# Attention in a two-layer kernel: transpositions by halves of 64 rows, scores three units ahead, maxima ahead of copies

## What is computed

```python
def _L0_attn_ref(x, ln_g, ln_b, w_qkv, w_out):
    h, dh, ws = (8, 64, 128)          # heads, head size, window; n = 256 tokens
    xn = layernorm(x) * ln_g + ln_b
    qk, v = jnp.split(xn @ w_qkv.T, 2, axis=-1)
    bq = rope(to_buckets(qk) * dh ** (-0.5))
    bk = rope(_look_around(to_buckets(qk), -1.0))
    bv = _look_around(to_buckets(v), -1.0)
    sim = jnp.einsum('bwie,bwje->bwij', bq, bk)
    sim = jnp.where(mask[None], NEG, sim)     # pads and |i - j| > 128 are masked
    attn = jax.nn.softmax(sim, axis=-1)
    out = jnp.einsum('bwij,bwje->bwie', attn, bv)
    return out @ w_out.T
```

## Time and profile before

| | |
|---|---|
| median of 3 runs | 978.69 us (976.3 to 979.37) |
| the profiled execution, its own time | 976.32 us |
| its span, first to last instruction | 975.0 us |
| PE busy | 952.0 us, 98% |
| DVE, ACT, POOL busy | 666.1, 505.4, 434.6 us |
| weight loads busy | 633.6 us |
| granted TensorE clock | 0.999 of full speed |

### The profile page before, as it was taken

The page is one execution under the profiler, slowest core; times in us unless marked ns, Lnnn a source line. Parts: engine busy times, 40 slices in busy tenths (PEclk is TensorE's granted clock), DMA queues, the critical chain, the costliest instruction groups (busy, mean ns, idle before and its releaser), DMA issues.

```text
span 975.0 us, 13550 instructions
## 1 busy us (share of the span) xinstructions
PE 952.0 (98%) x4508; PEld 633.6 (65%) x4508; DVE 666.1 (68%) x1578; ACT 505.4 (52%) x1165; POOL 434.6 (45%) x343
## 2 busy tenths in 40 slices
PE   5899999999999999999999999999999999999998
PEld 3565566676666766677666766667666676656765
DVE  6957769687665876767866677757777477724943
ACT  3574783536746266462764537545465454745222
POOL 5858247551094401863036620566206651054443
PEclk9999999999999999999999999999999999999999
DMA  7050240613423034230442306332053220543061
GB/s 284 12 174 1 35 130 0 144 44 10 133 68 98 22 13 133 72 93 21 38 129 76 88 1 91 76 95 68 1 99 90 65 66 2 107 102 87 23 164 33
DMA packets 63381, 72.80 MB, mean 75 GB/s; under 512 B 33288, under 2 KB 34312, under 8 KB 62928
## 3 DMA queue, kind: packets, MB, share of 16 engines
q1 hardware_dynamic: 61744, 69.81, 31.0%
q10 hardware_dynamic: 1568, 2.13, 0.6%
HBM read 69.04 MB, written 2.88 MB: 74 GB/s over the span
## 4 chain that ended last, share of the span: by engine, by line
PE 88%; DVE 7%; ACT 2%; issue 2%; DMA 0%; POOL 0%; DVEq 0%; ACTq 0%
PE ps L648 12%; PE ps L765 12%; PE ps L503 10%; PE ps L505 9%; PE ps L504 9%; PE ps L557 6%; PE ps L570 6%; PE ps L584 5%; PE ps L656 3%; PE ps L740 2%; PE ps L773 1%; PE ps L498 1%; PE ps L538 1%; PE ps L729 1%; PE ps L528 1%
## 5 line engine op out<-in xcount | busy, mean ns | idle before, releaser
L1167 ACT ACTIVATE wide<-ps 128x512 f32<-128x512 f32 x136 | 80.9, 595 | 208.8 <-PE ps L505 208.2
L1093 ACT ACTIVATE pw<-ps,w_cols 128x512 f32<-128x512 f32 x144 | 98.5, 687 | 98.6 <-PE ps L505 97.2
L1054 ACT ACTIVATE pw<-ps,nmax 128x256 f32<-128x256 f32 x256 | 117.5, 473 | 51.1 <-DVE nmax L1420 46.6
L648 PE MATMUL ps<-pw,w_w 128*128 128x512 f32 x288 | 135.4, 592 | 0.0
L1907 POOL TENSOR_TENSOR atc<-atc,wide 128x512 f32<-128x512 f32 x64 | 82.0, 1282 | 119.8 <-DVE atc L1634 119.8
L1887 POOL TENSOR_TENSOR kr<-qks,w_rope 128x512 f32<-128x512 f32 x32 | 43.8, 1367 | 158.3 <-DVE qks L1398 158.2
L1436 DVE COPY pt<-ps 128x512 f32<-128x512 f32 x126 | 81.7, 679 | 26.5 <-PE ps L570 26.3
L503 PE MATMUL ps<-yc,eg 128*128 128x512 f32 x128 | 94.4, 738 | 0.0
L1907 POOL TENSOR_TENSOR pt<-pt,wide 128x512 f32<-128x512 f32 x48 | 61.7, 1284 | 66.4 <-DVE pt L1634 65.3
L1420 DVE TENSOR_REDUCE nmax<-ps 128x4 f32<-128x1024 f32 (+1 forms) x80 | 79.1, 1006 | 13.8 <-PE ps L557 13.7
L648 PEld LDWEIGHTS ps<-pw,w_w 128*128 128x128 f32 x288 | 53.5, 189 | 42.6 <-issue 37.7
(11 more groups left out here) (229 smaller groups left out, 2131.0 us busy)
## 6 DMA issues: line engine op xcount, KB each, us to landing
wb<-scratch SPq DMA_DIRECT2D x128, 256.0 KB, 4.0
wb<-scratch SPq DMA_DIRECT2D x32, 512.0 KB, 5.9
wide<-scratch SPq DMA_DIRECT2D x16, 512.0 KB, 5.7
xin<-in_x SPq DMA_DIRECT2D x8, 256.0 KB, 2.7
out<-wide SPq DMA_DIRECT2D x7, 256.0 KB, 10.3
wb<-in_w SPq DMA_DIRECT2D x1, 1152.0 KB, 8.5
w_w<-in_w SPq DMA_DIRECT2D x1, 1152.0 KB, 12.4
w_ed<-in_ed SPq DMA_DIRECT2D x1, 1024.0 KB, 15.7
```

Source lines behind the costliest of these rows:

```text
L648: pe.matmul(bank(k), w2[:, e, c, :], hid[:, n % 4, :], start=c == 0, stop=c == 1 and e < E0).then_inc(*DOWN0.one)
L1054: m = act.activation(pw[:, u % 2, j, :], ps[:, score_bank(u, par), qt * SEQ:(qt + 1) * SEQ], ACT.Exp, bias=nmax[:, u % 3, j:j + 1], scale= ...
L1093: act.activation(hid[:, n % 4, :], bank(UPS0[n % 2]), ACT.Gelu, bias=cols[:, C_B1 + 2 * e + c:C_B1 + 2 * e + c + 1], scale=1.0).then_inc(* ...
```

## The change

In steps 2 to 7 (`s > 1`):

- **PE** turns units 0 to 6 by `turn_by_halves`: rows 0 to 63 of all eight 128 by 128 blocks of a unit go to bank 0 and rows 64 to 127 to bank 7, each a product with 64 rows and 64 moving columns, the two halves alternating. One event of two counts ends a unit. Unit 7 keeps `turn`.
- **PE's order**: `scores(2)` comes first, then for each unit its turn and `scores(u + 3)`; `weigh_pair` 0 and 1 stay ahead of turns 3 and 5; `weigh_pair` 2 comes behind the first `up0_half`, ahead of turn 7.
- **Masks**, in all steps: written by products of 64 rows, in the same halves of the array as the scores that follow. Each head's bank takes two such products, so `short_ident` and `mask` get a second copy, shifted by 64 columns, made at the start (`masks_further_on` on POOL, two more copies on ACT). `scores` now waits for both banks ahead of the first mask.
- **DVE**: `maxima(u + 2)` ahead of the copies of unit u. `pt_copy_half` copies a bank of one half into 64-wide pieces of `pt_of(u)`.
- **ACT**: `out_cols` of pairs 0 and 1 one unit later, behind units 4 and 6.

```diff
-        short_ident = sb("short_ident", [P, P], BF16)
-        mask = sb("mask", [P, 2, P], BF16)
+        short_ident = sb("short_ident", [P, 2, P], BF16)
+        mask = sb("mask", [P, 2, 2, P], BF16)
...
             def scores(s, u):
                 p, g = u // G, u % G
                 banks = [score_bank(u, par) for par in range(2)]
                 for b in banks:
                     take(b)
-                    pe.matmul(ps[:, b, P:3 * P], short_ident[:, :],
-                              mask[:, :, :].rearrange("p q k -> p (q k)"), start=True, stop=False,
-                              skip_group_check=True)
+                w.wait_ge(*MASKS.at(0))
+
+                for h in range(2):
+                    for par, b in enumerate(banks):
+                        rows = half_rows(par)
+                        pe.matmul(ps[:, b, P:3 * P], short_ident[rows, h, :],
+                                  mask[rows, h, :, :].rearrange("p q k -> p (q k)"), start=h == 0, stop=False,
+                                  skip_group_check=True)
...
+            def turn_by_halves(s, u):
+
+                for par, k in enumerate(TURN_BANKS):
+                    w.wait_ge(*EXPS.at(s, 2 * u + par))
+                    take(k)
+                for j in range(8):
+                    par, kt, qt = j // 4, j // 2 % 2, j % 2
+                    for h, k in enumerate(TURN_BANKS):
+                        m = pe.transpose(bank(k)[:, j * 64:j * 64 + 64],
+                                         pw[half_rows(h), u % 2, 2 * par + qt, kt * P:(kt + 1) * P],
+                                         ident[half_rows(h), half_rows(h)])
+                m.then_inc(TRANSPOSED.sem, 2)
+                for h, k in enumerate(TURN_BANKS):
+                    freed[k] = PT.at(s, 2 * u + h)
...
+                if s > 1:
+                    scores(s, 2)
+                    turn_by_halves(s, 0)
+                    rows1(s - 2, 1)
+                    scores(s, 3)
+                    for u in range(1, UNITS - 1):
+                        if u > 1 and u % G == 1:
+                            weigh_pair(s, u // G - 1)
+                        turn_by_halves(s, u)
+                        if u + 3 < UNITS:
+                            scores(s, u + 3)
+                    up0_half(s, E0, 0)
+                    weigh_pair(s, PAIRS - 2)
+                    turn(s, 7, 0)
+                    turn(s, 7, 1)
+                    up0_half(s, E0, 1)
...
-                    if u in (3, 5) and s > 1:
-                        out_cols(s, u // G - 1)
+                    if u in (4, 6) and s > 1:
+                        out_cols(s, u // G - 2)
...
-            act.activation(short_ident[:, :], ident[:, :], ACT.Identity).then_inc(*SHORT_IDENT.one)
+
+            act.activation(short_ident[:, 0, :], ident[:, :], ACT.Identity)
+            for h in range(2):
+                act.activation(short_ident[:, 1, (1 - h) * 64:(1 - h) * 64 + 64], ident[:, h * 64:h * 64 + 64],
+                               ACT.Identity).then_inc(*SHORT_IDENT.one)
...
+            def pt_copy_half(s, u, h):
+
+                w.wait_ge(*TRANSPOSED.at(s, 2 * u + 1))
+                if u >= 3:
+                    w.wait_ge(*WEIGHED.at(s, u - 3))
+                dve.tensor_copy(pt_of(u)[:, :, 64 * h:64 * h + 64],
+                                bank(TURN_BANKS[h]).rearrange("p (a q) -> p a q", q=64)).then_inc(*PT.one)
...
+                if s > 1:
+                    for u in range(UNITS):
+                        copied = pt_copy_half if u < UNITS - 1 else pt_copy
+                        if u + 2 < UNITS:
+                            maxima(s, u + 2)
+                        copied(s, u, 0)
+                        copied(s, u, 1)
+                        invert(s, u)
+                        if u == 1:
+                            out_rows(s - 2, 1)
...
-                own(pool.memset(mask[:, :, :], 0.0))
+                own(pool.memset(mask[:, :, :, :], 0.0))
...
+            def masks_further_on():
+
+
+                for qt, sign in enumerate((1, -1)):
+                    for b in range(2):
+                        part = mask[:, 1, qt, b * 64:b * 64 + 64]
+                        own(pool.affine_select(out=part, in_=part, compare_op=ALU.is_ge, fill=MASKED,
+                                               base=sign * (-64 if b == 0 else 0), pattern=[[-sign, 64]],
+                                               channel_multiplier=sign))
+                        side = 1 if b == 0 else -1
+                        m = pool.affine_select(out=part, in_=part, compare_op=ALU.is_ge,
+                                               fill=0.0 if (b == 0) == (qt == 0) else MASKED,
+                                               base=-64 if b == 0 else 63, pattern=[[0, 64]],
+                                               channel_multiplier=side)
+                m.then_inc(*MASKS.one)
...
             split_wv()
+            masks_further_on()
             rope_turn(0, 0)
```

More of the change, by code:

```diff
@@ L273, in two_layers @@
         STAGED = [semaphore(f"staged{k}") for k in range(2)]
-        CONSTANTS, IDENT, SHORT_IDENT = event("constants"), event("ident"), event("short_ident")
+        CONSTANTS, IDENT, SHORT_IDENT = event("constants"), event("ident"), event("short_ident", 2)
+        MASKS = event("masks")
         VARIANCE, RSTD = [event("variance0"), event("variance1")], [event("rstd0"), event("rstd1")]
@@ L541, in values, with half_rows @@
                 freed[k] = VALUE_ROWS.at(s, t)
+            def half_rows(h):
+                return slice(64 * h, 64 * h + 64)
             def scores(s, u):
@@ L781, in attention @@
                     scores(s, 1)
-                for u in range(UNITS):
+                if s > 1:
[14 more added lines that the diff above has]
+                    up0_half(s, E0, 1)
+                for u in range(UNITS if s < 2 else 0):
                     if u > 1 and second:
                         weigh(s, u - 1)
-                    if s > 1 and u > 1 and u % G == 1:
-                        weigh_pair(s, u // G - 1)
                     turn(s, u, 0)
@@ L791, in attention @@
                         rows0(0, VALUE_BANK)
-                    if u < 3 and s > 1:
-                        scores(s, u + 2)
                     turn(s, u, 1)
-                    if u == 0 and s > 1:
-                        rows1(s - 2, 1)
-                    if u < UNITS - 2 and (u > 2 or s < 2):
+                    if u < UNITS - 2:
                         scores(s, u + 2)
@@ L807, in attention @@
                         v1(0, 0, 5)
-                    if u == 6 and not second:
+                    if u == 6 and first:
                         up0_half(s, E0, 0)
-                    if u == 7 and not second:
+                    if u == 7 and first:
                         up0_half(s, E0, 1)
@@ L1650, in attention @@
                     rope_in(s, 3, 1)
-                for u in range(UNITS):
+                if s > 1:
[8 more added lines that the diff above has]
+                            out_rows(s - 2, 1)
+                for u in range(UNITS if s < 2 else 0):
                     pt_copy(s, u, 0)
-                    if u == 0 and s > 1:
-                        maxima(s, 2)
                     pt_copy(s, u, 1)
@@ L1657, in attention @@
                         x1_rows(0, VALUE_BANK)
-                    if u == 1 and s > 1:
-                        out_rows(s - 2, 1)
-                    if u and u < UNITS - 2 or u == 0 and s < 2:
+                    if u < UNITS - 2:
                         maxima(s, u + 2)
@@ L1869, in constants @@
                 pool.memset(half_power[:, :, :], -0.5)
-                own(pool.memset(mask[:, :, :], 0.0))
+                own(pool.memset(mask[:, :, :, :], 0.0))
                 for qt, sign in enumerate((1, -1)):
-                    m = pool.affine_select(out=mask[:, qt, :], in_=mask[:, qt, :], compare_op=ALU.is_ge,
+                    m = pool.affine_select(out=mask[:, 0, qt, :], in_=mask[:, 0, qt, :], compare_op=ALU.is_ge,
                                            fill=MASKED, base=0, pattern=[[-sign, P]],
```

## The result

The changed kernel takes 1003.82 us (median of 4 runs, 998.32 to 1007.21), the kernel before 978.13 beside it (976.30 to 979.37): 1.026 times as long, 95% interval 1.020 to 1.031. Forecast were 972.0 us, 966 to 982. The profiled execution took 1006.31 us, its span is 1005.0 against 975.0.

The account below looks back on a forecast made before the run. PE, 98% busy, was taken to bound the kernel, with DVE's little slack deciding the case. Gains of 5.8 us over six steps, 0.4 and 0.5 sum to 6.7: 978.69 - 6.7 = 972.0 us, range 966 to 982.

Parts of the forecast that it names:

- Part 4: Rest of the kernel: `out_cols` later gains 0.4 us, scores in the stage before 0.5; start work nothing; no DMA moved.
- 984.6: Rival: half-height loads in turns cost the ordinary 0.11 us a pair, +1.14 a step, kernel slower at 984.6; chance 0.17.
- 986: Rival: a pair's two loads run one after the other, 0.116 us, a turn takes 0.93, kernel 986 us; chance 0.05.
- Part 1: Turns by halves on PE: eight pairs at 0.058 us each, so a turn takes 0.46 in place of 0.87.
- Part 2: Masks in 64 rows: masks and scores behind a turn cost 1.08 us in place of 1.37, 0.10 more before `weigh`.
- Part 3, first stretch (8.03): Step 4, first turn to first `weigh`, with `scores(2)` put first: 0.58 us later than the 7.45 before.
- change of form: PE's extra cost of going from 128-row to 64-row products, 0.09 and 0.10 us, and of leaving again, 0.10.
- Middle (7.51): Step 4, first `weigh` to turn 5: 7.51 us in place of 8.38, earlier by 0.87.
- last (9.84): Step 4, turn 5 to L599, formerly 10.51 us: 0.67 earlier.
- about 0.05 back: Delay from the end of DVE's copies to PE's next turn, about 0.05 us within at least 2.05 turn to turn.
- The 0.8 us by which two attentions were longer: Two of six attentions ran 0.8 us longer; half, 0.4, was counted as gain from moving `out_cols` a unit later.
- Most of what PE saves turns into waiting: Of some 4.2 us a step taken off PE, three quarters, 3.2, becomes waiting for DVE's copies before turns.

Follow-up runs that it names:

- Experiment 1: Changed kernel with the expert weights stored as 128 contiguous rows of 32 values, not 4096 single 4-byte values (weights reach other tokens): 972.61 us, 0.995 of before.
- experiment 2: Kernel before with only the expert-weight store changed to 128 rows of 32 values (weights reach other tokens): 975.92 us, 0.9993 of before.
- 15: Changed kernel with weights stored in rows, plus a store just ahead of 4096 4-byte pieces of a constant that nobody reads: 1001.87 us, 1.024 of before.

## Why the prediction was wrong

The step that failed is Part 4's "No DMA is moved". It is true, and I took it to mean that no DMA bears on the change: the term stood at nothing, with no reason but this. Experiments 1, 2 and 15 show that a transfer that stays where it was costs 31 us once the engines beside it issue instructions more densely. In an attention PE issues 270 products and as many loads where it issued 203 and 202, sixteen within 0.49 us at a turn. No rival has this mechanism. The two that go that way, 984.6 and 986, have another cause, and the trace refutes it: their pairs would be 0.11 apart.

Without the burst the layout holds, and the gain in part. Experiment 1 takes 972.61 us, forecast 972.0; but the kernel before takes 976.27 beside it, so the gain is 3.7 (3.2 to 6.3 by the interval), forecast 6.7. Its profiled execution, the fastest of its four, has a span 5.9 shorter. PE's timeline of its middle stretch:

```profile
472.70 1.95 PE L608 MATMUL ps<-pt,vr 128*64 128x256 f32 x16
474.58 0.71 PE L592 MATMUL ps<-ident,pw 64*128 64x64 f32 x16
...
476.77 0.72 PE L592 MATMUL ps<-ident,pw 64*128 64x64 f32 x16 [0.39 <-DVE pt L1482]
...
480.38 0.71 PE L592 MATMUL ps<-ident,pw 64*128 64x64 f32 x16
482.57 0.72 PE L592 MATMUL ps<-ident,pw 64*128 64x64 f32 x16 [1.48 <-DVE pt L1482]
```

- *Part 1, the pair's price (0.058): right.* A turn of 16 lasts 0.66 to 0.71; less 0.22 for its last result that is 0.44 to 0.49 for fifteen starts, 0.059 to 0.065 a pair, a slow first one included. The Trainium skill's P / 1.2 ns for a load, which the forecast weighed, would make them 0.107; for these transpositions the trace disagrees. The range was misworked a little: 982 is reached at a pair price of 0.100, not 0.095, since 10.0 us over 6 steps of 5 turns of 8 pairs are 0.042 a pair.
- *Part 2, masks and scores: right.* In experiment 1 a turn at 470.97 is followed by `weigh` at 472.70, 1.73 us; forecast 0.52 + 1.08 + 0.10 = 1.70.
- *Part 3, first stretch (8.03): 8.06, in part by luck.* In experiment 1 the step starts at 464.64 and `maxima(2)` at 465.95, 1.31 later where I had 1.43: the masks and scores took 1.10 to the first turn, not 1.23, so the change of form was counted too dear. In return turn 2 starts 0.14 behind its copies (470.83, 470.97), not 0.05. The two errors cancel. Turns 1 and 2 wait 0.41 and 0.59, forecast 0.42 and 0.79.
- *Middle (7.51) and last (9.84): 0.17 and 0.07 too low*, 7.68 and 9.91. From turn to turn over DVE's copies it is 2.19, not 2.05. The term that was mis-sized is the "about 0.05 back": the copies at 475.33 end at 476.62, the turn starts at 476.77, 0.15 later. So 0.69 are gained a step, not 0.96, 4.1 us in six, not 5.8.
- *Part 4, the rest.* The 0.8 us by which two attentions were longer was not `out_cols` but the burst (experiment 2). The scores in the stage before gave 0.09 a step (the period fell by 0.78, from 118.12 to 117.34, the attention by 0.69), forecast 0.08.
- *Most of what PE saves turns into waiting: right.* L592 waits for the copies 17.2 us in experiment 1, 2.9 a step, forecast 3.2.

What stays open. The runs show that TensorE's increments, GpSimd's instructions and TensorE's fetches come late when the 4-byte writes and dense instructions meet; that all three queue at one place is my inference. Whether the increments themselves queue or the records from which the traces are made, these runs can't tell, since every execution was recorded. In the changed kernel 13 rises are missing, and with 8-byte pieces 3, while there hardly any time is lost; in the kernel before, with the burst, and in the runs with rows, none is. That fits full records, and excludes nothing. Nor is it settled what PE lacks in its four stops of 2.5 to 6.7 us, 18.0 in all. A fetch of 4.4 to 5.4 us overlaps the trouble in five of the six attentions; in step 4 it ends 4.2 us before PE goes on. The Trainium skill, Runtime: NRT & Kernel Launch, Instruction fetch mechanics, calls the cost of fetching the next block mostly hidden; without the burst that agrees with the traces, with it the fetches take 4.4 to 5.4 us, and that they cause the stops is only argued.

## What to carry to other kernels

Before an edit that packs more and shorter instructions into a stretch, look at what DMA does there, moved or not: a store of thousands of 4-byte pieces is the one to remove first. One 32x32-block transposition on VectorE made 128 rows of 128 bytes of it and turned 1003.8 us into 973.3. Where a trace shows "remote" releasers on one core or "issue" gaps on an engine that is full, compare ends of instructions with the rises of their semaphores before looking for the cause in the program's order. And where two banks are filled in turns, filling both at once takes from the reader its head start: here that ate most of what halved products gave.

## What the runs showed that I had not expected

- 4-byte writes from SBUF to memory: after about 2,500 in 1.5 us the rate falls to some 300 per us, and the store completes 17.7 us after its issue (step 4). 4096 pieces of 64 bytes keep 1,350 per us and are through after 3.1 us.
- From 7 us after the issue until the store is complete, increments of PE come up to 3.8 us late beside dense instructions, and a GpSimd that nobody waits for pauses 0.1 to 1.9 us between memsets that wait for nothing. No increment of DVE or ACT was seen late; some of their rises are missing from the trace.
- Two row halves side by side: transpositions of 64 rows and 64 columns run in pairs about 0.06 us apart, half of what a whole one takes.
- 2048 pieces of 8 bytes leave no late increment and 3 missing rises, and the time is within 0.2% of experiment 1's: half the pieces cost far less than half of the 31 us.
